# Reordered work at the front of the feed-forward and at the start of two Mamba layers

## The reference, cut to what matters

```
mod = silu(c) @ wmod            -> sa, ca, ga, sb, cb, gb          (a set for each block)
block 0:  h = layernorm(x) * (1+ca) + sa;  x += ga * additive_attention(h)
          h = layernorm(x) * (1+cb) + sb;  x += gb * fp4_ffn(h)    (128 -> 352 -> 128, fp4 rounding in blocks of 16)
block 1:  h = layernorm(x) * (1+ca) + sa
          for layer in 0, 1:                                       (Mamba)
              u, z = split(h @ W_in.T);  u = silu(conv4(u) + b)    (256 channels each)
              dt, B, C = split(u @ W_x.T);  dt = softplus(dt @ W_dt.T + b_dt)
              state[t] = exp(dt*A) * state[t-1] + dt*B*u           (16 states for each channel)
              h = (sum(state * C) + u*D) * silu(z) @ W_out.T
          x += ga * (h + residual)
          h = layernorm(x) * (1+cb) + sb;  x += gb * mixture_of_8_experts(h)
```

## Time and profile before

| | us |
|---|---|
| median of 3 runs | 755.59 (753.18 to 757.89) |
| the profiled execution, whole | 753.51 |
| its span, first to last instruction | 751.6 |
| attention and first feed-forward batch, about | 28 to 74 of the span |
| rest of the feed-forward | to 139 |
| start of layer 0, scan of layer 0 | 139 to 185, 185 to 368 |
| start of layer 1, scan of layer 1 | 368 to 413, 413 to 600 |
| router and experts | to 751.6 |

### The profile page before, as it was taken

How to read it: one execution, slowest core, us unless ns; L and a number is a source line. 1 busy time by engine, 2 the same in 40 slices (tenths; PEclk the granted TensorE clock), 3 DMA queues, 4 the chain that set the end, 5 groups by cost and what they waited for, 6 DMA issues and landing times. The chain is left out here.

```text
span 751.6 us, 8865 instructions
## 1 busy us (share of the span) xinstructions
PE 634.6 (84%) x2909; PEld 394.8 (53%) x2909; DVE 584.4 (78%) x820; ACT 497.2 (66%) x935; POOL 457.1 (61%) x259
## 2 busy tenths in 40 slices
PE   3955777688699999999988699999999972599992
PEld 2443455433455555555422455565655561499982
DVE  6794897557799999999765799999999958734521
ACT  3643534468999898989568999898989553033320
POOL 0136664100598989889600498989888615358866
PEclk9866788698799999999998699999999975599997
DMA  5000000001132323333001223232332181023323
GB/s 200 0 3 1 1 1 0 1 2 61 53 88 98 99 90 93 98 90 105 31 3 44 58 86 99 97 99 84 100 99 90 52 308 57 3 27 41 40 30 28
DMA packets 30780, 48.05 MB, mean 64 GB/s; under 512 B 3736, under 2 KB 12328, under 8 KB 30224
## 3 DMA queue, kind: packets, MB, share of 16 engines
q1 hardware_dynamic: 25600, 44.45, 18.4%
q0 software_dynamic: 5136, 3.05, 3.7%
HBM read 42.98 MB, written 4.49 MB: 63 GB/s over the span
## 5 line engine op out<-in xcount | busy, mean ns | idle before, releaser
L481 POOL TENSOR_TENSOR hc_all<-hs_all,c_row 128x1024 f32<-128x1024 f32 x87 | 205.0, 2369 | 122.0 <-DVE hs_all L1674 121.2
L1149 PE MATMUL ps<-hc_all,ident 128*128 128x512 f32 x508 | 237.1, 598 | 2.7 <-POOL hc_all L481 2.7
L1674 DVE TENSOR_TENSOR_SCAN hs_all<-da,ps 128x1024 f32<-128x1024 f32 x88 | 197.9, 2270 | 14.1 <-ACT da L811 9.1
L811 ACT ACTIVATE da<-big,a_neg 128x511 f32<-128x511 f32 x256 | 169.3, 709 | 30.7 <-DVE w_ffn L1674 29.1
L1149 PEld LDWEIGHTS ps<-hc_all,ident 128*128 128x128 f32 x508 | 90.2, 192 | 86.9 <-issue 77.0
L481 POOL TENSOR_TENSOR hc_all<-w_ffn,c_row 128x1024 f32<-128x1024 f32 x40 | 94.7, 2368 | 29.7 <-DVE w_ffn L1674 26.5
L1674 DVE TENSOR_TENSOR_SCAN w_ffn<-da,ps 128x1024 f32<-128x1024 f32 x40 | 91.4, 2285 | 3.8 <-ACT da L811 0.9
L1169 PE MATMUL ps<-ident,dbu 128*128 128x128 f32 x464 | 62.2, 279 | 11.2 <-ACT dbu L786 6.0
L1169 PEld LDWEIGHTS ps<-ident,dbu 128*128 128x128 f32 x464 | 54.2, 143 | 25.8 <-issue 18.7
L547 POOL DMA_INDIRECT out<-hc_all,hs_all x32 | 52.2, 1632 | 11.9 <-issue 8.8
L888 ACT ACTIVATE big<-ps,b 128x516 f32<-128x516 f32 x32 | 22.1, 690 | 47.3 <-PE ps L1340 47.3
(11 more groups left out here) (309 smaller groups left out, 1025.5 us busy)
## 6 DMA issues: line engine op xcount, KB each, us to landing
c_row<-c_rows SPq DMA_DIRECT2D x128, 256.0 KB, 3.1
tmpA<-w_in SPq DMA_DIRECT2D x2, 1024.0 KB, 7.2
tmpB<-w_in SPq DMA_DIRECT2D x2, 1024.0 KB, 9.3
x_tok<-x_in SPq DMA_DIRECT2D x2, 512.0 KB, 5.7
out<-x_tok SPq DMA_DIRECT2D x1, 1024.0 KB, 11.9
xm_rows<-xn SPq DMA_DIRECT2D x1, 1024.0 KB, 5.0
w_mod<-w_mod_in SPq DMA_DIRECT2D x2, 384.0 KB, 6.5
w_ffn<-w_ffn_in SPq DMA_DIRECT2D x1, 560.0 KB, 7.7
```

Source lines behind the costliest of these rows:

```text
L481: nc.gpsimd.tensor_tensor(hc[:, n % 4, :, :], hs3[HS_BUF[n]].rearrange("p (i s) -> p i s", i=IC), c_row[:, n % 4, :].unsqueeze(1).to_broad ...
L811: ins = nc.scalar.activation(da[:, n % 2, i, 1:S], dtT[:, b, i, 1:S], ACT.Exp, scale=a_neg[:, l, i, n:n + 1])
L1149: mm = nc.tensor.matmul(ps[:, YS + i, :], ident[:], hc[:, n % 4, i, :], start=(n == 0), stop=(n == NS - 1))
L1674: v.tensor_tensor_scan(hs3[HS_BUF[n]], decay, pair.rearrange("p i s -> p (i s)"), 0.0, ALU.mult, ALU.add).then_inc(c_scan, 1)
```

## The change

Nothing is computed differently; where and in which order it is done changes.

1. **Scores.** PE makes the key scores of batches 0 and 1 before the spread of the modulation, and those of 2 and 3 after it. DVE takes their maxima before it rounds the feed-forward weights, and ACT their exponentials before it copies the spread rows.
2. **First feed-forward batch.** DVE instead of POOL modulates batch 0 and multiplies the down weights by the gates, in 3 operations instead of 12. Block 1's modulation is made earlier on PE, ACT and DVE. The addition of the last attention batch into x stands behind the scales of the first feed-forward batch.
3. **Start of layer 0.** PE projects u of batch 0 after two batches are transposed (before: three), into banks 6 and 7; z of batch 0 goes to banks 4 and 5 before the last batch is transposed, and u and z of batch 1 follow without a wait for batch 0. ACT loads the SiLU table behind the modulation of the last batch.
4. **Start of layer 1.** POOL writes the zeros, and PE makes dt, B and C of batch 0 before u of batch 2.

```diff
-        U_BANK, Z_BANK = [[0, 0, 0, 0], [2, 2, 0, 0]], [[2, 2, 2, 2], [4, 0, 2, 2]]
+        U_BANK, Z_BANK = [[6, 0, 0, 0], [2, 2, 0, 0]], [[4, 2, 2, 2], [4, 0, 2, 2]]
...
             pool.wait_ge(mod_done, 2)
-            modulate_x(0)
             divide(q_x, 1, x_flat(0), 0)
             rescale(q_x, 1, x_flat(0), mag_x, 0)
 
-            pool.wait_ge(f_wT, 3)
-            for b in range(B):
-                for k, n in enumerate(KD):
-                    ins = nc.gpsimd.tensor_tensor(wd_gated[0:n, b, k, :], wdT[0:n, k, :], gates[0:n, 1, b, :], ALU.mult)
-                ins.then_inc(f_wd, 1)
...
+                if l + 1 < L:
+                    for k in range(2):
+                        pool.wait_ge(c_sum, NS * B - 2 + 2 * k)
+                        nc.gpsimd.memset(u_pad[:, k, :, 0:KC - 1], 0.0).then_inc(pad_ready, 1)
...
             magnitudes(q_x, 0, w_ffn[:], q_mag[:])
+            act.wait_ge(a_pooled, B)
+            exps(1, 0, 9)
             act.wait_ge(mod_bc, 1)
             nc.scalar.copy(gates[:, 0, :, :], ps[:, 0:B, 0:D]).then_inc(mod_done, 1)
-            act.wait_ge(a_pooled, B)
-            exps(1, 0, 9)
...
-            act.preload_act_table(ACT.Silu)
             modulated_second(2)
...
                             modulated_second(B - 1)
+                            act.preload_act_table(ACT.Silu)
...
+            def key_scores(g):
+                for b in range(2 * g, 2 * g + 2):
+                    pe.wait_ge(a_pooled, b + 1)
+                    pe.wait_ge(a_mkT, b + 1)
+                    pe.wait_ge(a_exp_s, b + 1)
+                    project(4 + b, a_score, wk_pooled[:, b, :], mkT[:, b * S:(b + 1) * S])
+
+            key_scores(0)
...
             mm.then_inc(mod_bc, 1)
...
+            key_scores(1)
             attended(0)
             attended(1)
...
             transposed_second(1)
-            transposed_second(2)
...
                 if l == 0:
                     project_in(0, 0, 0)
+                    transposed_second(2)
+                    project_in(0, 0, 1)
                     transposed_second(B - 1)
...
+                    if (l, b) == (1, 1):
+                        project_in(l, b + 1, 0)
...
+            pool_max(1, 0, 8)
             round_fp4(q_x, 0, w_ffn[:], q_mag[:])
-            pool_max(1, 0, 8)
             pool_max(1, 1, 8)
...
+            def modulate_first():
+                dve.wait_ge(f_xn, 1)
+                dve.wait_ge(mod_done, 2)
+                chain.link(v.tensor_tensor(x4[:, 0, :, :], x4[:, 0, :, :], scale_b[:, 0, :].unsqueeze(1).to_broadcast([P, TB, D]),
+                                           ALU.mult))
+                chain.link(v.tensor_tensor(x4[:, 0, :, :], x4[:, 0, :, :], shift_b[:, 0, :].unsqueeze(1).to_broadcast([P, TB, D]),
+                                           ALU.add))
...
+            add_attended(0)
+            add_attended(1)
+            inverses(0)
+            second_modulation()
+            add_attended(2)
...
+            modulate_first()
             scales_x(0)
...
+            add_attended(3)
             round_fp4(q_x, 1, x_flat(0), mag_x)
+            gated_down()
+            inverses(1)
...
-                if l:
-                    dve.wait_ge(c_sum, B * NS - 2)
-                    v.memset(u_pad[:, 0, :, 0:KC - 1], 0.0).then_inc(pad_ready, 1)
```

More of the change, by code:

```diff
@@ L654, in _ @@
             normalise_x(1)
-            deviations(1)
-            act.preload_act_table(ACT.Silu)
-            gate_rows(1, slice(4, 6), slice(0, 2))
-            magnitudes(q_x, 1, x_flat(0), mag_x)
             act.wait_ge(mod_bc, 2)
@@ L662, in _ @@
                            ps[:, 6:8, :].rearrange("p h (k g d) -> p h k g d", k=2, g=2)).then_inc(mod_done, 1)
+            magnitudes(q_x, 1, x_flat(0), mag_x)
+            deviations(1)
+            act.preload_act_table(ACT.Silu)
             evacuate_x(0)
@@ L1128, in _ @@
                         pe.wait_ge(q["m_u"], IC * b)
-                        if l and b == 1:
+                        if b == 1:
                             pe.wait_ge(q["m_z"], 1)
@@ L1516, in _, with add_attended @@
             value_weights(1)
-            for b in range(B):
+            def add_attended(b):
                 dve.wait_ge(a_out, b + 1)
@@ L1523, in _, with inverses, second_modulation, gated_down @@
                 layer_norm_stats(b * TB, TB)
[L1524 to L1528 removed]
+            def inverses(g):
+                ts = slice(2 * g * TB, (2 * g + 2) * TB)
+                dve.wait_ge(std_ready, 2 + g)
+                chain.link(v.reciprocal(rstd[:, ts], std[:, ts]))
+                v.scalar_tensor_tensor(nmr[:, ts], mv[:, ts, 0], -1.0, rstd[:, ts], ALU.mult, ALU.mult).then_inc(nmr_ready, 1)
+            def second_modulation():
+                dve.wait_ge(mod_raw, 2)
+                cols = ps[:, 7, 2 * D:2 * D + 4 * B].rearrange("p (j k b) -> p j k b", j=2, k=2)
+                own = mod_cols[:, 2:6, :].rearrange("p (j k) b -> p j k b", k=2)
+                v.tensor_copy(own[:, :, 0, :], cols[:, :, 0, :])
+                v.tensor_scalar(own[:, :, 1, :], cols[:, :, 1, :], 1.0, None, ALU.add).then_inc(mod_col, 1)
+                gate_signs(1, slice(4, 6))
+            def modulate_first():
[5 more added lines that the diff above has]
+                                           ALU.add))
+            def gated_down():
+                dve.wait_ge(f_wT, 3)
+                for k, n in enumerate(KD):
+                    ins = v.tensor_tensor(wd_gated[0:n, :, k, :], wdT[0:n, k, :].unsqueeze(1).to_broadcast([n, B, D]),
+                                          gates[0:n, 1, :, :], ALU.mult)
+                ins.then_inc(f_wd, 1)
+            add_attended(0)
[3 more added lines that the diff above has]
+            add_attended(2)
             def scales_x(b):
[L1531 removed]
+                after(dve, f_h, b)
                 dve.wait_ge(q_x["q_done"], b + 1)
@@ L1592, in _ @@
             normalise_batch(1)
+            inverse(4, 2)
+            normalise_batch(2)
+            v.memset(u_pad[:, :, :, 0:KC - 1], 0.0).then_inc(pad_ready, 1)
             add_down(2 * B - 1)
             second_stats(3)
-            for b in range(2, B):
-                inverse(4, b)
-                normalise_batch(b)
+            inverse(4, 3)
+            normalise_batch(3)
             for l in range(L):
```

44 lines of the change are left out of this document (14 added, 30 removed).

## The result

The changed kernel takes 744.79 us (median of 4 runs, 742.91 to 751.35) against 755.16 for the kernel before on the same chip; the ratio is 0.9893, 95% interval 0.985 to 0.9936. The profiled execution took 743.85, its span 742.1. Forecast were 749.2 and a range of 744.5 to 753.

A forecast was written before the change was run, and what follows sets the result against it. Chains of waits between engines, not a full engine, were taken to set the pace at both layer starts and from 28 to 75 us. Terms +0.4 - 5.2 - 1.55 = -6.35 us gave 749.2 us, range 744.5 to 753.

The forecast's parts named there:

- Part 1: Attention scores ahead of the spread: DVE and POOL collide more, so value_weights ends later, +1.7 us (bounds -3.1 to +2.8).
- The sign of 51 to 53: Trace sign that the forecast is right: the first addition into x starts at 51 to 53 us.
- The sign I had named: Trace sign in value_weights: L1486's counterpart and the small products take over 1 us more often than once.
- Rival A: Attention front: POOL's additions no longer collide with value_weights, first addition into x before 49, total about 745 us; chance 0.2.
- Rival B: Attention front: PE's clock falls, last scores 3 us later, front +2.4 to +3 instead of +0.4, total 751.5 us; chance 0.13.
- Part 2: First feed-forward batch, to the first hidden product: terms of +0.1, -1.2 and -0.2 us, together -1.3.
- The middle and the end of the feed-forward: Same instructions in the same order, so a shift passes through unchanged; counted as zero.
- Part 3: Start of layer 0: ACT's first dt copy comes 5.2 us earlier (bounds -3.4 to -5.9).
- From there on the loop is the same: Layer 0 after the first dt copy: the loop to the first scan is unchanged, counted as zero.
- Part 4: Start of layer 1: first dt copy some 2.6 us earlier, second 1.55; counted as -1.55 (bounds 0 and -2.6).
- The experts: Stage from the last scan to the end: same instructions in the same order, counted as zero.
- Rival D: Rest of the feed-forward: shifted DVE and POOL phase adds 8 x 1.1 = 8.8 us, total 758 us; chance 0.05.

The follow-up runs named there:

- the second comparison: The changed kernel and the kernel before, both unaltered, run again on one chip: 747.75 us against 757.8, ratio 0.9878.
- e6_table_early: The changed kernel with the SiLU table load back at its old place, ahead of ACT's modulation of the third batch; 742.96 us, ratio 0.9861.
- e8_layer1_old: The changed kernel with the old start of layer 1 (u of batch 2 before dt, B and C; DVE writes the zeros); 746.17 us, ratio 0.988.
- e5_pool_modulates: The changed kernel with POOL again modulating the first feed-forward batch and gating the down weights; 744.5 us, ratio 0.986.
- e3_scores_behind: The changed kernel with all four scores behind the modulation's spread again and the weights rounded ahead of the maxima; 744.54 us, ratio 0.9872.
- e10_spread_late_free: The changed kernel with PE's second spread waiting for POOL's division and ACT's magnitudes ahead of its wait for the spread; 751.83 us, ratio 0.9931.

## Why the prediction was right, and where its sum was off

The forecast was a gain of 6.35 us; the medians show 8 to 10 (755.16 less 744.79 is 10.4, the ratio makes it 8.1, and that of the second comparison 9.2). The range held it, at its lower edge (744.79 for 744.5). That the sum came this near is in part luck: stages counted at zero gave -3.44, and others counted at zero took back 2.58 and 1.38.

- **Part 1, +1.7: right in kind, too large.** Measured +0.83, and 50.81 to 51.02 in two profiles against 49.63 and 50.19. The sign of 51 to 53 was met by 0.02 only; e6_table_early and e8_layer1_old, with the same instructions there, have 50.16 and 50.20. I counted two collisions in excess of before; there was one (0.73). The sign I had named (more than one operation of value_weights over 1 us) didn't show: one took 1.63, one 0.89. Of the 0.83, 0.73 are that one collision, of an operation with two inputs in SBUF beside POOL's addition, as the Trainium skill's rule (SBUF — State Buffer, the two separate sides) has it. Rival A (additions before 49) fell. Rival B's mechanism, the clock, is there: the last scores end at 40.3 in the changed kernel (clock 0.50) and at 37.3 in e6_table_early (1.00), with the same instructions there. But its price isn't 2.4 to 3: where the weighted sums began 2.8 us earlier (e6_table_early, 40.04 for 42.88), six operations of DVE were held up by POOL's additions instead of four, and the first addition came only 0.9 earlier. POOL's end, not the scores', is what is late there.
- **Part 2, -1.3: right.** Measured -1.43: -0.96 up to the transposes of x and -0.47 behind them, of which 0.32 is the clock (the first gate and up products took 4.72 for 5.04). But it is one mechanism of two halves, as e5_pool_modulates showed.
- **"The middle and the end of the feed-forward ... a shift passes through them unchanged": wrong.** This is the step that failed. -3.44 us in the profiles; 61.3 us in five profiles with the new front, 63.3 to 64.7 in the three with the old one, and 62.2 to 65.8 in the six with the new front and a further edit there. PE isn't busiest there, but its products lie in the chain, and they have two durations. Which of them holds in the first two pairs was changed by the place of the spread (1.0 to 1.3 us, shown); for the rest of the 3.44 the new front is the likely reason, not a shown one, and 1.2 us of it is the base, which took 63.56 the second time.
- **Part 3, -5.2: too small, and given back in part.** -6.46 at the first dt copy; 14.46 to 14.48 us in eight profiles with the new order, 16.75 in one (e3_scores_behind, where the products for u of the third batch took 3.68 at a clock of 0.53, for 1.98). The projections took 1.88 where I had taken 2.3, and the copy of u came at 138.08, 1.1 us sooner after the last down product than reckoned. One part of the change neither its description nor my sum names: DVE now normalises the third batch ahead of the last addition of the feed-forward. PE waited 2.47 us for that batch before (141.73, 2.92 behind the last down product) and doesn't now (136.77, 2.00 behind it); without it up to 0.9 us of the gain would be gone, an estimate from these rows. No run tests it alone. The table's load fits the sum (its 1.28 on the path); at its old place, in e6_table_early, 0.74 of it came back. "From there on the loop is the same" was wrong as the line above: it took 27.74 instead of 25.16, in the second half of the loop (8.05 and 8.27 from dt copy to dt copy for 6.69 and 7.05), and e5_pool_modulates shows 25.18 for the same instructions. Net, to the first scan, -3.88 against the first profile of before, -7.7 against the second.
- **Part 4, -1.55: right at the place, too small in the end.** -2.59 and -1.41 at the two copies for -2.6 and -1.55. I stopped at the second batch; the third gave 1.35 more, which is the clock once more and here always the same.
- **The experts**, counted at zero, are the largest spread: 157.06 to 162.91 us from the last scan to the end, independent of every edit. The traces say where it lies: POOL's indirect transfers, 32 of one line (L545 in the changed kernel) and 14 of another (L524), were busy for 66.3 us together where the stage took 157.1, for 68.1 where it took 158.5 and for 72.4 where it took 162.9, and without them the stage took 90.4 to 91.2 us in all 14 profiles. Why the transfers differ stays open; no run tests it. It is why the time of a single profile tells little of effects below 3 us.
- Rival D (slower by a shifted phase of DVE and POOL in the pairs) didn't come. A phase did shift there, of PE's clock, and with the other sign.

What stays open is why layer 0's loop keeps nearly its full clock in some executions (25.16 to 25.18 us in three profiles, granted 0.94 to 0.95) and not in others (27.7 or more, 0.83 in the changed kernel), and how much of the time's spread from run to run comes from it. The second profile of the kernel before, with 28.54 at 0.84, shows that the loss needs no change at all.

## What to carry to other kernels

Where PE's products lie in a chain of waits, a shift doesn't pass through a stage unchanged: price each such stage at both durations of its products and look at what PE does right ahead of it. Here it paid to move a spread of products with few rows away from the entry of a loop in which PE's products are waited for; but expect a gain bought by keeping PE busy at one point to be given back at the next. And take two or three profiles of the kernel before as the base: the one I had was 3.8 us shorter than the next in the stage on which most of the sum rested.

## What the runs showed of the hardware

- PE's products between waits have two durations: 2.60 and 5.03 us for eight of 128x352, 1.98 and 3.56 for four of 128x512. They follow the granted clock (1.00 and 0.53 in the stretches of the first, 1.00 and 0.54 over the second), that is the levels of 2.4 and 1.2 GHz. Groups in which the clock changes lie between (4.22 at 102.43 in the changed kernel, clock 0.59; 2.73 at 162.65, clock 0.69). In e10_spread_late_free the clock was low in PE's idle time from 59 to 63 (0.55), through the spread's 3.75 us (0.50) and on to 90.3 (0.50).
- A stage's length takes few discrete values: from the second to the third dt copy of a layer 6.7 or 8.05 to 8.1 us in all 14 profiles, from the first dt copy of layer 0 to its first scan 25.16 to 25.18, 27.74 to 27.82, or 28.2 to 29.4.
- POOL's 32 indirect transfers were busy for 52.2 us in five profiles and for 54.0 or 54.1 in nine, the 14 of another line for 14.1 to 18.4, with no relation to the edits. The five are those with the shortest last stage (157.06 to 157.61 us); the nine took 158.51 to 162.91.
